# Third attention with scores first in a tick, second and last attention with the later weights split in eight pieces

## Chip, cores and metric

One core of a Trainium2 chip. The metric is the device time of one execution in microseconds: the median of the runs shown, and beside it one execution taken with the hardware profiler, on which all rows below rest. One launch computes everything.

## What is computed

The kernel runs twelve layers on an activation x of 64 sequences of 32 tokens with 256 features: four rounds of cross-attention, self-attention and feed-forward network. Each layer adds its result to x; all but the first pass of x are normalized (mean and variance over the 256 features) before a layer. The change touches three self-attentions. Each has 16 heads of 64 features:

```python
q = x @ Wq; k = x @ Wk; v = x @ Wv            # 256 -> 1024, all three
# second attention (l1a): biases on q, k, v and the output, causal mask
# third attention (l2a): own normalization gain and offset, q and k brought to length 1 in each head,
#   times a scale for each feature, scores times 8, a distance bias, causal,
#   two constant keys and values for each head ahead of the 32 tokens
# last attention (l3a): plain, softmax with 1e-10 added to the sum
scores = q k^T * scale ; p = softmax(scores) ; x = x + (p v) @ Wo
```

## The kernel before, in words

TensorE, VectorE, ScalarE, GpSimd and the SyncE queue each run a program written out by hand; they meet in semaphores only. x lies in the on-chip memory as 16 tiles of 128 tokens (four sequences each). A weight or activation that enters a precise product is taken apart in an upper part (rounded, written by ScalarE with `copy_act`) and a lower part (the difference, written by VectorE with a subtraction), and `three` issues three products for one: upper by upper, lower by upper, upper by lower.

**Ticks.** A layer's stages are ordered by `ticks(n, stages, order)` (L87): in tick t it calls, in the order of the list, each stage for tile t minus its lag; the lag is the key or the first entry of the key. Each engine has a list of its own. A wait blocks everything behind it on its engine.

**Banks.** `Banks.take` hands out PSUM banks in rotation; who takes a bank first waits until its contents of before have been read (`freed`). In the three attentions two banks rotate; scores have two banks of their own and values four.

**SelfAttention** (L899 to L1104), p is the lag of the scores: scores at p (TensorE); top at p on VectorE (mask, maximum, subtraction: L1034, L1039, L1041); exponential at p + 2 (ScalarE); divide at p + 3 (VectorE: L1047, L1052, L1054, then 32x32 turnings L1059, L1060); constant at p + 4 (TensorE, L976, third attention only: products of the constant values); values at p + 4 (TensorE, L991), then their result copied by ScalarE (first half of the heads, upper part) and VectorE (`outT`: L1070, L1074, L1076); project at p + 5 (TensorE, 24 products with the output weights), and total at p + 5 (VectorE: addition to x, L389, with statistics L374, L378), which also frees the bank of the projection. In the third attention the lower part of the values' result has a single buffer: `outT` waits for the projection of the tile before it, ahead of L1074.

**wide_attn** (L1246) is the second (`l1a`) and the last (`l3a`) attention, p = 2. Its weights come in seven loads; q and k are taken apart between the four groups of the normalization (`norm.act`, `norm.dve` with `upper` and `lower` as `between`, four units: two halves of q, two of k). Then each of ScalarE and VectorE takes apart the two halves of v (128x1024), ScalarE also the output weights (128x2048), before its first tick; VectorE's lower part of the output weights stands in `row` (tick 1). Two tiles make one group u for the products: `p1` with part "a" and "b" at lag 0 gives q in tick 2u and k in tick 2u + 1, two banks of 12 products for each part, and at lag 4 v. `evict` copies them out: in the second attention ScalarE the even and VectorE the odd banks of q and k (L1395, L1397), in the last the other way round (L200, L1393).

**l2_attn** (L1448) is the third attention, p = 3. For tile i, p1 "q" and "k" (lag 0) make q and k, two banks of 6 products each, p1v (lag 4) v, p2 "q" and "k" (lag 2) turn them on TensorE with the identity (L1548), constant at lag 7, values 7, project 8. VectorE at lag 0: copies q with its offset (L1646), sums of squares (L1649); GpSimd: `roots` (L1588, L1590), a power of -1/2; VectorE `p1b` at lag 1: q and k times the roots, one instruction (L1656, which the trace names g_xn); at lag 2 it copies the first half of the turned q and k (L1662), ScalarE the second (L1707); ScalarE also copies k (L200) and squares (L1696). TensorE's list is

```python
[(2, "q"), 3, (2, "k"), (7, "constant"), 8, (0, "k"), 7, (4, "v"), (0, "null"), (0, "q")]
```

VectorE's is `[2, 3, 8, 1, 6, (0, "k"), 7, (0, "q"), (0, "later")]`, where 3 is top, 8 total, 1 p1b, 6 divide, 7 outT.

## Time and profile before

| | |
|---|---|
| median of 3 runs | 3779.59 us (3779.45 to 3786.15) |
| profiled execution | 3792.68 us, span 3790.9 us |
| TensorE busy | 3426.5 us (90%), 39372 matmuls |
| VectorE busy | 2143.7 us (57%) |
| ScalarE busy | 1278.9 us (34%) |
| GpSimd busy | 900.4 us (24%) |
| granted clock of TensorE, mean | 0.938 |
| second attention | about 857 to 1122 us of the span |
| third attention | about 2108 to 2493 us |
| last attention | about 3489 to 3755 us |

A busy share is an average over twelve layers with different limits. A granted clock of 1.0 is the upper of TensorE's two levels (2.4 GHz), 0.5 the lower (1.2 GHz). Names: psum is the PSUM; l1a_, l2a_, l3a_ mark the tiles of the three attentions; g_ those of all layers.

### The profile page before, as it was taken

The numbers are of one execution on the slowest core, as the hardware profiler recorded it, in microseconds if no ns is written. First come the engines' busy times: TensorE is split into PE (matmuls) and PEld (weight loads), VectorE is DVE, ScalarE is ACT, GpSimd is POOL, SyncE is SP. The second block draws the span as 40 slices with busy tenths as digits, with TensorE's granted clock in tenths as the row PEclk, the third lists the DMA queues.
The fourth block names the chain that finished last, engine by engine and source line by source line (L and its number), as shares of the span: only waits on it lengthen the run. The fifth ranks groups of instructions, "written<-read, shape, count | busy, mean of one in ns | idle before, by whom it ended". The sixth has DMA issues, their size and how long they took to land.

```text
span 3790.9 us, 92569 instructions
## 1 busy us (share of the span) xinstructions
PE 3426.5 (90%) x39372; PEld 2774.3 (73%) x39372; DVE 2143.7 (57%) x5316; ACT 1278.9 (34%) x3193; POOL 900.4 (24%) x1393
## 2 busy tenths in 40 slices
PE   7988749988998889999999789889999999998996
PEld 6876647547986667777777577778888777776895
DVE  5756553356665165555555567654444466666467
ACT  5863101323212223333333443232232244445111
POOL 6657124122022332222222333100000111001102
PEclk9989769999997989999999899989999999998997
DMA  5620248531021321111110100021221111111000
GB/s 155 183 72 3 92 150 269 166 125 47 3 79 63 88 77 46 46 46 46 47 48 19 54 2 3 3 91 62 89 73 62 46 41 38 38 39 58 3 3 26
DMA packets 209995, 246.43 MB, mean 65 GB/s; under 512 B 18132, under 2 KB 189904, under 8 KB 206640
## 3 DMA queue, kind: packets, MB, share of 16 engines
q1 hardware_dynamic: 202096, 230.27, 19.1%
q0 software_dynamic: 7488, 10.23, 1.5%
q8 instruction: 313, 5.13, 0.5%
q14 instruction: 98, 0.80, 0.1%
HBM read 221.46 MB, written 18.61 MB: 63 GB/s over the span
## 4 chain that ended last, share of the span: by engine, by line
PE 71%; DVE 15%; issue 6%; ACT 3%; POOL 3%; DMA 1%; SPq 0%; ACTq 0%; POOLq 0%; DVEq 0%
PE psum L189 44%; PE psum L3621 10%; PE psum L991 2%; DVE l3x_P L3966 2%; PE psum L3100 1%; PE psum L963 1%; PE psum L3862 1%; PE psum L3201 1%; PE psum L3169 1%; PE psum L976 1%; DVE l3x_V L3949 1%; DVE l2a_ss L1649 1%; POOL l0a_ms L1191 1%; PE psum L3110 1%; DVE g_xn L258 1%
## 5 line engine op out<-in xcount | busy, mean ns | idle before, releaser
L3621 PE MATMUL psum<-l2f_hhi,l2f_whi 128*128 128x512 f32 x512 | 199.2, 389 | 0.0
L3621 PE MATMUL psum<-l2f_hlo,l2f_whi 128*128 128x512 f32 x512 | 199.2, 389 | 0.0
L3621 PE MATMUL psum<-l2f_hhi,l2f_wlo 128*128 128x512 f32 x512 | 199.2, 389 | 0.0
L245 POOL TENSOR_SCALAR g_rs<-g_mv 128x4 f32<-128x4 f32 x24 | 5.2, 218 | 778.2 <-DVE g_mv L378 777.7
L189 PE MATMUL psum<-l2x_kT,l2x_Qp 128*128 128x257 f32 x768 | 179.2, 383 | 2.6 <-ACT g_xn L3513 2.6
L189 PE MATMUL psum<-g_xn,l2x_tok 128*128 128x384 f32 x512 | 177.7, 489 | 1.4 <-ACT g_xn L3522 1.4
L189 PEld LDWEIGHTS psum<-l2x_kT,l2x_Qp 128*128 128x128 f32 x768 | 142.0, 191 | 21.7 <-issue 3.0
L3675 DVE CAST l2f_hhi<-l2f_tmp 128x512 fp32r<-128x512 f32 x96 | 41.0, 427 | 201.4 <-ACT l2f_tmp L3738 200.3
L189 PEld LDWEIGHTS psum<-g_xn,l2x_tok 128*128 128x128 f32 x512 | 93.3, 190 | 56.9 <-issue 2.6
L3949 DVE COPY l3x_V<-psum 128x512 f32<-128x512 f32 x64 | 44.3, 691 | 159.6 <-PE psum L189 159.6
L389 DVE TENSOR_TENSOR g_x<-g_x,psum 128x256 f32<-128x256 f32 x128 | 53.0, 415 | 132.2 <-PE psum L189 129.1
L3738 ACT ACTIVATE l2f_tmp<-psum,g_cols 128x512 f32<-128x512 f32 x64 | 44.2, 690 | 240.1 <-PE psum L3621 240.1
L200 ACT ACTIVATE l2x_Pc<-psum 128x384 f32<-128x384 f32 x128 | 62.8, 492 | 183.9 <-PE psum L189 183.9
L4022 ACT ACTIVATE l3x_P<-psum,l3x_sm 128x257 f32<-128x257 f32 x256 | 117.5, 469 | 16.0 <-DVE l3x_sm L3958 15.9
L189 PE MATMUL psum<-l3x_ctxT,l3x_wk 128*128 128x256 f32 x512 | 121.4, 380 | 0.0
L189 PE MATMUL psum<-l3x_wv,l3x_ctxT 128*128 128x256 f32 x512 | 121.0, 379 | 0.0
L3513 ACT ACTIVATE g_xn<-psum,l2x_sm 128x257 f32<-128x257 f32 x192 | 89.0, 472 | 90.8 <-DVE l2x_sm L3422 90.8
L3415 DVE TENSOR_REDUCE l2x_sm<-psum 128x3 f32<-128x771 f32 x64 | 61.5, 961 | 102.2 <-PE psum L189 102.2
L3621 PEld LDWEIGHTS psum<-l2f_hlo,l2f_whi 128*128 128x128 f32 x512 | 96.1, 188 | 20.2
L3621 PEld LDWEIGHTS psum<-l2f_hhi,l2f_whi 128*128 128x128 f32 x512 | 96.1, 188 | 19.9
L3621 PEld LDWEIGHTS psum<-l2f_hhi,l2f_wlo 128*128 128x128 f32 x512 | 96.1, 188 | 19.9
L200 ACT ACTIVATE l3x_PT<-psum 128x512 f32<-128x512 f32 x64 | 38.3, 598 | 207.4 <-PE psum L3862 207.4
(854 smaller groups left out, 10079.2 us busy)
## 6 DMA issues: line engine op xcount, KB each, us to landing
l2f_raw<-L2f_h SPq DMA_DIRECT2D x64, 512.0 KB, 3.2
l0f_w<-L0f_w SPq DMA_DIRECT2D x23, 1024.0 KB, 8.0
l0x_ctxT<-ctxT SPq DMA_DIRECT2D x64, 257.0 KB, 2.8
l1x_ctxT<-ctxT SPq DMA_DIRECT2D x64, 257.0 KB, 6.0
l0x_ctok<-ctx SPq DMA_DIRECT2D x64, 256.0 KB, 3.0
l1x_ctok<-ctx SPq DMA_DIRECT2D x64, 256.0 KB
l2x_cT<-ctxT SPq DMA_DIRECT2D x64, 256.0 KB, 2.7
l2x_tok<-ctx SPq DMA_DIRECT2D x128, 128.0 KB, 2.8
```

The lines of the kernel that those rows point to most:

```text
L189: ins = e.matmul(out, lhsT, rhs, start=start and n == 0, stop=stop and n == len(pairs) - 1, skip_group_check=skip)
L200: return e.activation(out, in_, ACT.Copy)
L389: e.tensor_tensor(K.x[:, i, :], K.x[:, i, :], part, ALU.add).then_inc(*K.sig("x").up())
L991: t = e.matmul(self.o_bank[j][par * hd:(par + 1) * hd, ch * 32:ch * 32 + 32], v[s, b * hd:(b + 1) * hd], PT[s, par * nch + ch, :], start=n ...
L3415: e.tensor_reduce(m(0), rows[:, :, 0:257], AX.X, ALU.max).then_inc(*s_top.up())
L3513: t = e.activation(P[k][:, n, :], bank[n][:, 0:257], ACT.Exp, bias=sm[:, k, 2, n:n + 1], scale=0.125, accum_out=sm[:, k, 3, n:n + 1])
L3621: t = e.matmul(z, a, b, start=c == 0 and u == 0, stop=c == 7 and u == 2)
L3675: e.tensor_copy(h[0][:, m, :], u[:]).then_inc(*h_hi.up())
L3738: e.activation(tmp[n % 4][:], banks.of(("m", g, n))[:], ACT.Gelu, scale=K.col(("L2_ffn_h1_s", "L2_ffn_h2_s")[n // 8], n % 8)).then_inc(*ge ...
L3949: e.tensor_copy(V[b % 6][:], banks.of(("v", b))[:].rearrange("p (k d) -> p k d", k=2)).then_inc(*v_ok.up())
L3966: t = e.tensor_scalar(P[b % 3][:, r, :], P[b % 3][:, r, :], m(0)[:, r:r + 1], None, ALU.mult)
L4022: e.activation(P[k][:, r, :], bank[r][:, 0:257], ACT.Exp, bias=sm[:, k, 1, r:r + 1], scale=0.25, accum_out=sm[:, k, 2, r:r + 1]).then_inc( ...
```

## The change

Three edits.

In the second and last attention the units of v and of the output weights become eight pieces of 512 columns (one `c` of the two, one half of the columns), and the engines take them apart inside the ticks: `later` calls `upper` or `lower` for two pieces in each of ticks 0 to 3, one after the first copies of products ("c"), one at the end of the tick ("d"). The loads stay as they were; the waits for the pieces (`w_lo.at(...)`) are counted anew.

In the third attention the lists of TensorE, VectorE and ScalarE are put in another order, and VectorE's copies of the turned q and k become two stages.

```diff
-        units = [(n, slice(h * 512, (h + 1) * 512)) for n in "qkv" for h in range(2)] + [("o", slice(0, 1024))]
+        half = [slice(h * 512, (h + 1) * 512) for h in range(2)]
+        units = [(n, slice(0, 2), half[h]) for n in "qk" for h in range(2)] + [(n, slice(c, c + 1), h) for n in "vo" for h in half for c in range(2)]
...
-                    w.wait_ge(w_lo.at(n // 2 + 1 if n < 8 else 5 + n % 2))
+                    w.wait_ge(w_lo.at(n // 2 + 1 if n < 8 else 6 + 2 * (n % 2)))
...
-            n, cols = units[u]
+            n, c, cols = units[u]
             w.wait_ge(w_hi.at(u + 1))
-            e.tensor_tensor(W[n][1][:, :, cols], raw[n][:, :, cols], W[n][0][:, :, cols], ALU.subtract).then_inc(*w_lo.up())
+            e.tensor_tensor(W[n][1][:, c, cols], raw[n][:, c, cols], W[n][0][:, c, cols], ALU.subtract).then_inc(*w_lo.up())
...
-            copy_act(e, W[n][0][:, :, cols], raw[n][:, :, cols]).then_inc(*w_hi.up())
+            copy_act(e, W[n][0][:, c, cols], raw[n][:, c, cols]).then_inc(*w_hi.up())
...
-        at.wo_ok = w_lo.at(7)
+        at.wo_ok = w_lo.at(12)
...  VectorE
-            for u in (4, 5):
-                lower(e, w, u)
+            def later(i, part):
+                if i < 4:
+                    lower(e, w, 4 + 2 * i + part)
...
-                lower(e, w, 6)
...
-            ticks(16, {**evict(e, w, banks, "dve"), (1, "row"): row, **at.dve(e, w, banks)}, [2, (0, "a"), (4, "a"), 5, 6, 7, (0, "b"), (4, "b"), (1, "row")])
+            ticks(16, {**evict(e, w, banks, "dve"), (1, "row"): row, (0, "c"): lambda i: later(i, 0), (0, "d"): lambda i: later(i, 1),
+                       **at.dve(e, w, banks)}, [2, (0, "a"), (4, "a"), (0, "c"), 5, 6, 7, (0, "b"), (4, "b"), (1, "row"), (0, "d")])
...  ScalarE
-            for u in (4, 5, 6):
-                upper(e, w, u)
...
+                  [(4, "power"), (0, "a"), (4, "a"), (0, "c"), 6, (0, "b"), (4, "b"), (0, "d")])
...  third attention, TensorE
-                  [(2, "q"), 3, (2, "k"), (7, "constant"), 8, (0, "k"), 7, (4, "v"), (0, "null"), (0, "q")])
+                  [3, (2, "q"), (7, "constant"), (2, "k"), 7, 8, (0, "k"), (4, "v"), (0, "null"), (0, "q")])
...  VectorE (p2 now takes q or k by its second argument)
-                  [2, 3, 8, 1, 6, (0, "k"), 7, (0, "q"), (0, "later")])
+                  [(2, "q"), 3, (2, "k"), 1, 7, 8, 6, (0, "k"), (0, "q"), (0, "later")])
...  ScalarE
-                       **at.act(e, w, banks)}, [2, 5, (0, "k"), 7, (4, "v"), (0, "q"), (0, "later")])
+                       **at.act(e, w, banks)}, [2, 5, 7, (0, "k"), (4, "v"), (0, "q"), (0, "later")])
```

## Rows read from the trace of the kernel before

**Rows 1.** The page: the chain that ended last, share of the span by engine.

```profile
PE 71%; DVE 15%; issue 6%; ACT 3%; POOL 3%; DMA 1%; SPq 0%; ACTq 0%; POOLq 0%; DVEq 0%
```

**Rows 2.** Table by windows: stretch, length, busy PE, PEld, DVE, ACT, POOL, PE clock, DMA.

```profile
2339.06:2358.59 19.53, 18.32 (x396) 15.62 (x396) 14.76 (x25) 7.46 (x12) 5.73 (x2) 1.00 0.01 3
```

**Rows 3.** Timeline of TensorE, one tick: start, length, instruction, idle before it.

```profile
2339.68 0.66 PE L1548 MATMUL psum<-g_ident,g_xn 128*128 128x128 f32 x4 [1.07 <-DVE g_xn L1646]
...
2341.73 1.09 PE L1548 MATMUL psum<-g_ident,g_xn 128*128 128x128 f32 x8 [0.17 <-DVE l2a_qT L1662]
...
2347.59 0.39 PE L189 MATMUL psum<-l2a_wkhi,g_xT_parts 128*128 128x512 f32 x1
...
2348.99 0.39 PE L189 MATMUL psum<-l2a_wkhi,g_xT_parts 128*128 128x512 f32 x1
...
2351.90 0.50 PE L189 MATMUL psum<-l2a_wvhi,g_xT_parts 128*128 128x512 f32 x1
```

**Rows 4.** Timeline of VectorE over the same tick.

```profile
2336.83 0.75 DVE L1646 SCALAR_TENSOR_TENSOR g_xn<-psum,l2a_qs,l2a_bq 128x512 f32<-128x512 f32 x1
...
2343.09 0.78 DVE L1034 SCALAR_TENSOR_TENSOR l2a_P<-psum,l2a_alibi 128x272 f32<-128x272 f32 x2
...
2347.79 0.42 DVE L389 TENSOR_TENSOR g_x<-g_x,psum 128x256 f32<-128x256 f32 x1 [2.41 <-PE psum L189]
...
2348.55 2.26 DVE L1656 TENSOR_TENSOR g_xn<-g_xn,l2a_ss 128x2048 f32<-128x2048 f32 x1
2350.72 0.71 DVE L1047 TENSOR_REDUCE l2a_nm<-l2a_P 128x16 f32<-128x544 f32 x1
...
2354.40 0.68 DVE L1070 CAST l2a_oThi<-psum 128x512 fp32r<-128x512 f32 x1
...
2356.37 0.75 DVE L1646 SCALAR_TENSOR_TENSOR g_xn<-psum,l2a_qs,l2a_bq 128x512 f32<-128x512 f32 x1
```

**Rows 5.** Timeline of GpSimd over the same tick.

```profile
2341.10 0.29 POOL L1588 TENSOR_SCALAR l2a_ss<-l2a_ss 128x32 f32<-128x32 f32 x1 [13.70 <-DVE l2a_ss L1649]
2341.47 5.44 POOL L1590 TENSOR_TENSOR l2a_ss<-l2a_ss,g_negh 128x32 f32<-128x32 f32 x1
```

**Rows 6.** Timeline of GpSimd, other ticks, and the table by windows over one.

```profile
2190.52 5.44 POOL L1590 TENSOR_TENSOR l2a_ss<-l2a_ss,g_negh 128x32 f32<-128x32 f32 x1
2204.22 5.46 POOL L1590 TENSOR_TENSOR l2a_ss<-l2a_ss,g_negh 128x32 f32<-128x32 f32 x1
...
2239.18 5.45 POOL L1590 TENSOR_TENSOR l2a_ss<-l2a_ss,g_negh 128x32 f32<-128x32 f32 x1
2261.18 5.44 POOL L1590 TENSOR_TENSOR l2a_ss<-l2a_ss,g_negh 128x32 f32<-128x32 f32 x1
...
2240.00:2260.00 20.00, 18.31 (x269) 15.62 (x268) 13.06 (x20) 6.77 (x11) 4.63 (x1) 0.91 0.01 2
```

**Rows 7.** Second attention: timelines of TensorE, ScalarE, VectorE, and one window.

```profile
874.54 0.55 PE L189 MATMUL psum<-g_xT_parts,l1a_wqhi 128*128 128x256 f32 x1 [6.98 <-ACT l1a_q L1395]
...
868.28 2.03 ACT L200 ACTIVATE l1a_wvhi<-l1a_wv 128x1024 fp32r<-128x1024 f32 x2
...
873.57 0.82 ACT L1395 ACTIVATE l1a_q<-psum,g_cols 128x256 f32<-128x256 f32 x2
...
870.60 2.35 DVE L1367 TENSOR_TENSOR l1a_wv_parts<-l1a_wv,l1a_wvhi 128x1024 fp32r<-128x1024 f32 x2
...
874.50:879.10 4.60, 4.56 (x22) 4.59 (x23) 0.00 (x0) 0.84 (x2) 0.00 (x0) 0.52 0.00 0
```

**Rows 8.** Last attention: timelines of VectorE and TensorE, and one window.

```profile
3502.13 2.35 DVE L1367 TENSOR_TENSOR l3a_wv_parts<-l3a_wv,l3a_wvhi 128x1024 fp32r<-128x1024 f32 x2
...
3505.23 0.55 PE L189 MATMUL psum<-g_xT_parts,l3a_wqhi 128*128 128x256 f32 x1 [6.04 <-DVE l3a_q L1393]
...
3505.20:3510.60 5.40, 5.37 (x25) 5.40 (x26) 0.69 (x1) 1.26 (x2) 0.00 (x0) 0.50 0.00 0
```

**Rows 9.** Waits in 2105 to 2500 us: engine, line, releaser, total, times, longest.

```profile
PE psum L976 <- DVE l2a_oTlo L1076: 9.7, 4, 4.0
```

More of the change, by code:

```diff
@@ L1293, in sp @@
             mark["w"] = wt.now()
-            for u, (n, cols) in enumerate(units[:6]):
+            for u in range(6):
+                n, cols = "qkv"[u // 2], half[u % 2]
                 load(e, w_in[u], raw[n][:, :, cols], A[pre + "_" + n].rearrange("(c p) m -> p c m", p=128)[:, :, cols])
@@ L1363, in lower @@
         def lower(e, w, u):
-            n, cols = units[u]
+            n, c, cols = units[u]
             w.wait_ge(w_hi.at(u + 1))
-            e.tensor_tensor(W[n][1][:, :, cols], raw[n][:, :, cols], W[n][0][:, :, cols], ALU.subtract).then_inc(*w_lo.up())
+            e.tensor_tensor(W[n][1][:, c, cols], raw[n][:, c, cols], W[n][0][:, c, cols], ALU.subtract).then_inc(*w_lo.up())
         def upper(e, w, u):
-            n, cols = units[u]
-            w.wait_ge(w_in[u].at(2 if n == "o" else 1))
-            copy_act(e, W[n][0][:, :, cols], raw[n][:, :, cols]).then_inc(*w_hi.up())
-        at.wo_ok = w_lo.at(7)
+            n, c, cols = units[u]
+            w.wait_ge(w_in[6].at(2) if n == "o" else w_in[2 * "qkv".index(n) + cols.start // 512].at(1))
+            copy_act(e, W[n][0][:, c, cols], raw[n][:, c, cols]).then_inc(*w_hi.up())
+        at.wo_ok = w_lo.at(12)
         def evict(e, w, banks, mine):
@@ L1432, in act, with later @@
             w.wait_ge(L("cols").at(0))
-            for u in (4, 5, 6):
-                upper(e, w, u)
-            ticks(16, {**evict(e, w, banks, "act"), **{(4, "power") if k == 4 else k: f for k, f in at.act(e, w, banks).items()}}, [(4, "power"), (0, "a"), (4, "a"), 6, (0, "b"), (4, "b")])
+            def later(i, part):
+                if i < 4:
+                    upper(e, w, 4 + 2 * i + part)
+            ticks(16, {**evict(e, w, banks, "act"), **{(4, "power") if k == 4 else k: f for k, f in at.act(e, w, banks).items()},
+                       (0, "c"): lambda i: later(i, 0), (0, "d"): lambda i: later(i, 1)},
+                  [(4, "power"), (0, "a"), (4, "a"), (0, "c"), 6, (0, "b"), (4, "b"), (0, "d")])
         K.layer(sp, pe, pool, dve, act)
@@ L1656, in p1b, with p2 @@
                 e.tensor_tensor(d, d, f.unsqueeze(2).to_broadcast([128, 32, 64]), ALU.mult).then_inc(*qn_ok.up())
-            def p2(i):
-                for n in (0, 2):
+            def p2(i, a):
+                for n in [2 * a]:
                     w.wait_ge(turned.at(4 * i + n + 1))
-                    o = (qT[i % 2][:].rearrange("p c (j q) -> p c j q", j=4), kT[i % 2][:, :, :, 2:34])[n // 2]
+                    o = (qT[i % 2][:].rearrange("p c (j q) -> p c j q", j=4), kT[i % 2][:, :, :, 2:34])[a]
                     e.tensor_scalar(o[:, 0:4], banks.of(("T", i, n))[:].rearrange("p (c j q) -> p c j q", c=4, j=4),
                                     K.col(("L2_attn_q_scale", "L2_attn_k_scale")[n // 2], 0), None, ALU.mult).then_inc(*T_dve.up())
-            ticks(16, {(0, "q"): lambda i: p1(i, 0), (0, "k"): lambda i: p1(i, 1), 1: p1b, 2: p2,
-                       (0, "later"): later, **at.dve(e, w, banks)},
-                  [2, 3, 8, 1, 6, (0, "k"), 7, (0, "q"), (0, "later")])
+            ticks(16, {(0, "q"): lambda i: p1(i, 0), (0, "k"): lambda i: p1(i, 1), 1: p1b,
+                       (2, "q"): lambda i: p2(i, 0), (2, "k"): lambda i: p2(i, 1), (0, "later"): later, **at.dve(e, w, banks)},
+                  [(2, "q"), 3, (2, "k"), 1, 7, 8, 6, (0, "k"), (0, "q"), (0, "later")])
         def act(e):
```

## Prediction

> **What bounds the kernel now.** I read the page first, then split the stage of the third attention (2105 to 2493 us of the span) into its ticks with the table by windows, then the timelines of VectorE, TensorE and GpSimd over one tick, and last the first microseconds of the second and the last attention. The chain that ended last is mostly TensorE [rows 1], so a change counts where it moves TensorE's waits. A full tick of the third attention takes 19.53 us, of which TensorE is busy 18.3 and VectorE 14.8, at the full clock (2.4 GHz) [rows 2]. TensorE's two waits in it are 1.07 us, before the second half of the turning of q, for VectorE's copy of q's second half, and 0.17 us before the turning of k [rows 3]. Its work without them is 19.53 - 1.07 - 0.17 = 18.3 us.
>
> In the second attention TensorE stands 6.98 us after its first 24 products, until ScalarE's copy of q ends [rows 7]; in the last it stands 6.04 us, until VectorE's [rows 8]. In both cases the copy is late because the engine first takes apart all the later weights.
>
> **Third attention, part by part.** The change moves work only; no instruction is added here, and no DMA moves. On TensorE scores now stand ahead of the turning of q (they last about 1.3 us, the time between the turnings that start at 2339.68 and 2341.73 less the first of them and the wait [rows 3], and so cover the 1.07), the constant part stands between the turnings (it covers the 0.17), and values come ahead of the output projection. If nothing else waited the tick would be 18.3 us.
>
> But VectorE's order changes too: the big multiplication by the roots (L1656), then the three copies of the values' result, then the addition to x (L389). Before, the addition came ahead of the multiplication, 2347.79 against 2348.55 [rows 4]. The multiplication needs GpSimd's roots, and these end at 2341.47 + 5.44 = 2346.91 [rows 5], 1.64 us before it began: not waited for today. And the addition frees the bank (there are two) which the second half of k's product takes: banks are taken as q, q, k, k (turnings), y, k, k, v, v, q, q, so that product takes y's bank. The new order closes a loop over four engines. Its length, from the rows:
> - second half of k's product to the first copy of q: 2356.37 - 2348.99 = 7.38, less the values, which move out of it, 2351.90 - 2348.99 - (2348.99 - 2347.59) = 1.51: 5.87 us [rows 3, 4];
> - first copy of q to the start of the roots, 2341.10 - 2336.83 = 4.27, and to their end 5.81 more [rows 4, 5];
> - multiplication until the next instruction starts, 2350.72 - 2348.55 = 2.17; copies of the values' result, 2356.37 - 2354.40 = 1.97; the addition 0.42 [rows 4]; some 0.13 for three signals between engines.
> Sum 5.87 + 4.27 + 5.81 + 2.17 + 1.97 + 0.42 + 0.13 = 20.64 us against 19.54: +1.1 us per tick, and TensorE's stand moves to the second half of k's product, where it is 20.64 - 18.3 = 2.3 us. VectorE itself stands some 2.3 us for the roots in the same tick. Eight ticks have both a k and a y (8 to 15): 8 x 1.1 = **+8.8 us**.
>
> First ticks. Where no y is taken yet, k's product takes the bank of the turned k, which VectorE now copies after the mask, maximum and subtraction (2.3 us: from 2343.09 to 2347.79 less the 2.41 of standing [rows 4]) instead of before. Chain from the first copy of q: 4.1 to the copy of the turned q, which starts just before the roots' 4.27; 0.7 + 2.3 + 0.75 for it, the softmax's top and the turned k's copy; then k, v and half of q at 1.40 us a half: 5 x 1.40, and 0.25 for signals: 15.1 us. The shortest such tick now is 2204.22 - 2190.52 = 13.7 us [rows 6]. Of the five ticks 3 to 7 I count two as bound so, those with v and without divide and values; in the others something else is as long: 2 x 1.4 = **+2.8**, between 0 (if the mask waits are shorter) and 7 (all five).
>
> Last ticks (16 to 23). Today TensorE stands up to 4.0 us for the lower copy of the values' result [rows 9]. In the new order that copy waits, with its single buffer, for the projection before it, which is now issued after values; so 1.3 us of it come into each of some five ticks, less one projection that no longer waits at the very end (3.3), and less 0.65 a tick of the copy's first part that gets out of the chain. Bounds -3 and +6, taken **+3**, nearer to the chain's rows. Sum for the third attention +14.6.
>
> TensorE's clock. One of the eight ticks took 22.0 us instead of 19.54 (roots at 2239.18 and 2261.18), with a granted clock of 0.91 over it: part of it ran at the lower level (1.2 GHz) [rows 6]. A slow stretch that falls between scores and the first half of k would now be covered by the 2.3 us stand; against that, the new stand may bring slow stretches of its own. I let the two cancel, with -4 and +11 as bounds.
>
> **Second attention.** ScalarE now ends its part of the normalization at 868.28, where it began the v weights, and copies q at once instead of at 873.57 [rows 7]. The copy frees TensorE 0.97 us after its start: 869.25 instead of 874.54. The next half waits for VectorE, which is free at 870.60: copy 0.85 as ScalarE's, so 871.5, and 24 products end by 873.0. Before, they began at 874.54 and, at the lower clock (0.52 in the row that covers them), ended at 879.1 [rows 7]. Gain 6.1. The later stages are bound by TensorE, so it stays. The single piece of 2.3 us that delays the first softmax afterwards becomes 0.7: 0.4 more. **-6.5 us.**
>
> **Last attention.** VectorE copies q where it began the two v pieces (3502.13), and not after them: 2.3 us of 2.35 [rows 8]. The first 24 products after the stand took 5.4 us at a granted clock of 0.50 [rows 8], 2.8 at the full one. With a stand of 3.8 instead of 6.0 us the fall may or may not come: 0 to 2.5, taken 1.0. **-3.3 us**, between -2.3 and -4.8.
>
> The pieces: eight of 512 columns where there were two of 1024 and one of 2048. Two of 1024 take 2.35 us on VectorE [rows 7], so a piece of 512 costs at most half a 1024 and its fixed part, some 0.7: 5.5 against 4.6 us, in stretches where TensorE is behind with the products that VectorE copies. A piece waits for ScalarE's, and behind it stand a copy and then the softmax; the copy has the length of a half product (1.4) to spare. Cost 0, at worst 0.5 a tick over four ticks in two stages, +4.
>
> **Sum.** +14.6 - 6.5 - 3.3 = +4.8 us, against the profiled execution's 3792.7 (span 3790.9): 3797.5. The runs' median stands 13 us lower, and I carry the difference over: 3779.6 + 4.8 = **3784 us**.
>
> **Rivals.**
> Scores first pays in full: the roots are not in the loop (GpSimd's spans are rough), or the addition to x does not hold k's bank. Then ticks of 18.3: 8 x -1.2, and -3 at the end, -12.6 in all, -22.4 with the other stages: 3757 us. For it: VectorE has 4.7 us to spare in a tick [rows 2]. Against it: five ticks show the same 5.44 to 5.46 us for the roots [rows 5, 6].
>
> Slower by the clock. This is the case that ends on the other side of no change. The place is the second half of k's product: TensorE stands 2.3 us there in one piece, and v and q come next. It decides if that stand, once a tick, lets the clock fall: then the products behind it, which are in the loop, lose 1.4 us on average a tick, 8 x 1.4 = +11: 3795 us. For it: the tick of 22.0 us [rows 6]; against it: with a stand of 1.07 the clock was 1.00 [rows 2]. The Trainium skill ("TensorE: Matmul & The Clock Gate", section on a second failure mode, PSUM-queue depth-cycling) says that short stands between groups of products, made by cycling through PSUM banks, can make the clock oscillate; by it this case would be the likeliest.
>
> The pieces do little: copies are held up behind them and the clock falls in the last attention all the same. Then 5 us are gained there and not 9.8: 3789 us.
>
> **How the numbers follow.** Forecast 0.60 (a total between 3776 and 3792 by the bounds), scores pay 0.12, clock 0.15, pieces 0.13. About 0.2% (7.6 us) is what a measurement of this kernel can tell from no change. Faster by more: the second case, and 0.02 of the first: 0.14. Slower: clock 0.15, half of the pieces' case, and 0.13 of the forecast's own: 0.35. Within: 0.51. The range 3769 to 3796 leaves out most of the second case and the end of the third.
>
> **What would show it.** In ticks 8 to 15 of the third attention: start to start 20.6 us; TensorE waits some 2.3 us at a product of k for VectorE's addition L389, none for L1646; VectorE's L1656 waits some 2.3 us for GpSimd. In the second attention TensorE's first stand 2 us and a second of 0.9, in the last 3.8. Wrong, if the ticks are 18.3 or over 21.5 us, or L1656 is not waited for.

## The result: 0.34% slower, and the profile after

The changed kernel takes 3795.0 us (median of 17 runs, 3786.17 to 3808.68) against 3781.4 us for the kernel before measured beside it (17 runs, 3773.79 to 3790.45). The ratio is 1.0034, 95% interval 1.0025 to 1.0044: slower by 9 to 17 us. The forecast was 3784 us in a range of 3769 to 3796, so the time lies inside the range, but only 1 us from its upper end, and on the side that had a chance of 0.35; that no change beyond the noise would be seen had been the likelier case, with 0.51.

The profiled execution of after (span 3786.8 us) happens to be shorter than that of before (3790.9 us), and this must not be read as a gain. The code that neither kernel changed took 2890.6 us in the profile of before and 2878.1 us in that of after; in the fourteen profiles of this study it lies anywhere from 2874.3 to 2890.6 us. So I compare the three stages themselves. Each is measured by the starts of two instructions that are in every trace:

| stage, from and to | before | after | difference |
|---|---|---|---|
| second attention: first product of q to the logits' addition | 864.5 to 1135.4: 270.9 | 855.0 to 1117.7: 262.7 | -8.2 |
| third attention: first roots to the last addition to x (L389) | 2130.3 to 2490.9: 360.6 | 2112.2 to 2495.35: 383.1 | +22.5 |
| last attention: first product of q to the first instruction on l3f_wi | 3496.1 to 3764.9: 268.8 | 3497.9 to 3760.8: 262.9 | -5.9 |
| the rest of the span | 2890.6 | 2878.1 | -12.5, by chance |

The three stages add up to +8.4 us in this pair of profiles. A second profile of after, taken on another chip (run e8 below), has 262.9, 388.3 and 265.4 us: +16.3. The measured 9 to 17 us lie around these. The stages scatter too: the third attention took 383.1 and 388.3 us in the two profiles of after, and 356.4 to 363.8 us in the five profiles with the old order (before, e2, e10, e11, e12), so a single pair of profiles is good to some 5 to 7 us only.

The page's chain of after, to be read against [rows 1] (shares of the span by engine):

```profile
PE 73%; DVE 15%; issue 4%; POOL 4%; ACT 3%; DMA 1%; SPq 0%; ACTq 0%; DVEq 0%; POOLq 0%
```

GpSimd went from 3 to 4% of the chain: its roots (L1600) are now on it, with 2%.

Two ticks of the third attention after, by the table by windows (stretch, length, busy PE, PEld, DVE, ACT, POOL, granted clock, DMA), cut at the starts of the roots, as an answer to [rows 2]:

```profile
2250.10:2272.10 22.00, 19.70 (x404) 16.66 (x403) 14.75 (x24) 7.44 (x12) 5.73 (x3) 0.92 0.01 2
...
2316.40:2337.00 20.60, 18.27 (x407) 15.55 (x403) 14.69 (x25) 7.44 (x12) 5.75 (x2) 1.00 0.01 2
2337.00:2359.10 22.10, 19.80 (x404) 16.68 (x404) 14.67 (x25) 7.44 (x12) 5.72 (x2) 0.92 0.01 2
2359.10:2379.80 20.70, 18.42 (x408) 15.61 (x404) 14.78 (x25) 7.44 (x12) 5.75 (x2) 1.00 0.01 2
```

There are two kinds of full ticks, and a first one apart. Where the granted clock is 1.00 over the whole tick it takes 20.6 us, the length of the loop that the prediction worked out (20.64). Where it is 0.92, TensorE does the same work in 19.8 instead of 18.3 us and the tick takes 22.1 us: the whole 1.5 us is paid. The first full tick, 22.92 us, is another matter: over it the clock was 0.81 and TensorE busy for 22.5 us, so it hardly stood at all, and its low clock set the tick; the low clock came at the start, 0.55 over the first 9.7 us. Over the eight full ticks the starts of the roots are 22.92, 21.99, 22.17, 22.05, 20.62, 22.15, 20.64 and 20.61 us apart (before: 22.00, 21.68, 19.55, 19.54, 19.52, 19.54, 19.53, 19.86).

The loop itself can be followed in the timeline of one such tick after (start, length, engine, line, instruction, idle before it and what ended it), which answers to [rows 3], [rows 4] and [rows 5]. TensorE's rows first:

```profile
2357.05 1.09 PE L1558 MATMUL psum<-g_ident,g_xn 128*128 128x128 f32 x8
2358.08 1.99 PE L976 MATMUL psum<-l2a_PnT,l2a_nv 32*128 32x32 f32 x64
2359.99 1.09 PE L1558 MATMUL psum<-g_ident,g_xn 128*128 128x128 f32 x8
...
2369.27 0.50 PE L189 MATMUL psum<-l2a_wkhi,g_xT_parts 128*128 128x512 f32 x1 [1.44 <-DVE g_x L389]
```

VectorE and GpSimd over the tick:

```profile
2358.64 0.74 DVE L1672 TENSOR_SCALAR l2a_qT<-psum,g_cols 128x512 f32<-128x512 f32 x1
2359.18 5.46 POOL L1600 TENSOR_TENSOR l2a_ss<-l2a_ss,g_negh 128x32 f32<-128x32 f32 x1
...
2364.67 2.29 DVE L1666 TENSOR_TENSOR g_xn<-g_xn,l2a_ss 128x2048 f32<-128x2048 f32 x1 [2.42 <-POOL l2a_ss L1600]
2366.88 0.68 DVE L1070 CAST l2a_oThi<-psum 128x512 fp32r<-128x512 f32 x1
2367.60 0.69 DVE L1074 TENSOR_TENSOR l2a_oTlo<-psum,l2a_oThi 128x512 fp32r<-128x512 f32 x1
2368.20 0.68 DVE L1076 TENSOR_TENSOR l2a_oTlo<-psum,l2a_oThi 128x512 fp32r<-128x512 f32 x1
2368.80 0.41 DVE L389 TENSOR_TENSOR g_x<-g_x,psum 128x256 f32<-128x256 f32 x1
...
2375.18 0.75 DVE L1656 SCALAR_TENSOR_TENSOR g_xn<-psum,l2a_qs,l2a_bq 128x512 f32<-128x512 f32 x1 [1.89 <-PE psum L189]
```

What the change set out to do is there: the two turnings have no wait in front of them, and the constant's products lie between them. Then VectorE stands 2.42 us for GpSimd's roots, works without a gap through multiplication, three copies and addition, and only when the addition has run does TensorE go on with the second half of k's product (2369.27; the stand is 1.44 us here, with another of 0.84 us earlier in the tick, ahead of the projection, and 2.30 in one piece in the tick before). That product leads to the next copy of q (2375.18), and this one to the next roots: the loop is closed.

In the four ticks at 0.92, and in e1's two, the clock falls at the end of this stand or within 1.2 us behind it. Four stretches of after by the table by windows: in the tick of 22.1 us TensorE is idle, then 2 us later at the lower clock; in the tick of 20.6 us before it the same stand is followed by the upper clock:

```profile
2345.00:2347.00 2.00, 0.00 (x0) 0.00 (x0) 1.97 (x5) 1.06 (x2) 0.00 (x0) 1.00 0.00 0
2349.00:2352.00 3.00, 3.00 (x9) 2.32 (x8) 2.08 (x5) 1.63 (x3) 0.00 (x0) 0.50 0.00 0
```

```profile
2324.00:2326.00 2.00, 0.16 (x1) 0.00 (x0) 1.97 (x4) 1.23 (x2) 0.00 (x0) 1.00 0.00 0
2328.00:2331.00 3.00, 3.00 (x14) 2.44 (x13) 2.47 (x5) 1.84 (x4) 0.00 (x0) 1.00 0.00 0
```

The list of waits of after over 2100 to 2510 us (engine, line, releaser, total, times, longest; PEld is TensorE's loading of weights, which meets the same stand):

```profile
DVE g_xn L1666 <- POOL l2a_ss L1600: 39.2, 16, 5.3
...
PEld psum L189 <- DVE g_x L389: 22.1, 12, 2.8
PE psum L189 <- DVE g_x L389: 16.9, 12, 2.3
...
PE psum L976 <- DVE l2a_PT L1060: 11.9, 4, 4.7
```

In the same list of before there is no wait of TensorE's product for L389 at all, and VectorE waited for the roots 6 times, 12.7 us. The four waits of [rows 9], for the lower copy of the values' result, are gone, and four for the turned softmax weights (L1060), of up to 4.7 us, stand in their place.

The second attention after, timelines of ScalarE, VectorE and TensorE, against [rows 7]:

```profile
858.11 0.87 ACT L1397 ACTIVATE l1a_q<-psum,g_cols 128x256 f32<-128x256 f32 x2
...
860.43 0.87 DVE L1399 TENSOR_SCALAR l1a_q<-psum,g_cols 128x256 f32<-128x256 f32 x2
861.22 0.68 DVE L1369 TENSOR_TENSOR l1a_wv_parts<-l1a_wv,l1a_wvhi 128x512 fp32r<-128x512 f32 x1
861.35 0.38 PE L189 MATMUL psum<-g_xT_parts,l1a_wqhi 128*128 128x256 f32 x1 [0.58 <-DVE l1a_q L1399]
```

And the last attention after, TensorE, against [rows 8]:

```profile
3504.00 0.36 PE L189 MATMUL psum<-g_xT_parts,l3a_wqhi 128*128 128x256 f32 x1 [1.01 <-DVE l3a_q L1395]
```

The stands of 6.98 and 6.04 us have shrunk to 0.58 and 1.01 us. Here the first 24 products of q ran partly at the lower clock (0.50 over the first 2 us in the second attention and the first 4 us in the last), and covered part of the wait themselves; in runs where they ran at the full clock the stands are 1.7 and 0.6 us in the second attention and 3.76 us in the last (below).

One part of the old stand is not a conversion. ScalarE, which TensorE waited for in the second attention, itself stood for the load of the output weights before it took them apart, between the v weights of [rows 7] and its copy of q:

```profile
871.76 1.91 ACT L200 ACTIVATE l1a_wohi<-l1a_wo 128x2048 fp32r<-128x2048 f32 x1 [1.45 <-DMA l1a_wo<-L1a_o]
```

So of the 5.3 us by which the copy came later than ScalarE could have begun it, 1.45 were a wait for a transfer. Putting the weights off takes this wait out of the way as well.

### The profile page after: what moved, and what is told of

Its sections match the earlier page's. It is cut to its first block, busy times and chain, and to the rows that moved or that the text cites. A ratio compares the mean times of both kernels' runs of the same rounds, so it can differ in the third digit from the quotient of the medians.

```text
span 3786.8 us, 92604 instructions
## 1 busy us (share of the span) xinstructions
PE 3414.4 (90%) x39372; PEld 2763.8 (73%) x39372; DVE 2145.4 (57%) x5326; ACT 1279.3 (34%) x3203; POOL 901.6 (24%) x1393
## 4 chain that ended last, share of the span: by engine, by line
PE 73%; DVE 15%; issue 4%; POOL 4%; ACT 3%; DMA 1%; SPq 0%; ACTq 0%; DVEq 0%; POOLq 0%
PE psum L189 46%; PE psum L3631 10%; PE psum L991 2%; DVE l3x_P L3976 2%; POOL l2a_ss L1600 2%; PE psum L963 1%; PE psum L3110 1%; PE psum L3872 1%; PE psum L3211 1%; PE psum L3179 1%; DVE l3x_V L3959 1%; DVE g_xn L258 1%; POOL l0a_ms L1191 1%; PE psum L3120 1%; PE psum L3111 1%
## 5 line engine op out<-in xcount | busy, mean ns | idle before, releaser
L3924 POOL COPY l3x_kT<-l3x_kTt 128x2 f32<-128x2 f32 x64 | 12.3, 192 | 402.8 <-PE psum L3863 392.4
```

## The experiments

They go from the change's two halves (e1, e2) to the loop (e3 to e5), to better orders (e6, e7), to a repeat of the whole (e8), to the clock (e9), and to what in the pieces does the work (e10 to e12). Every ratio is to the kernel before, run beside it on the same chip.

**e1: only the third attention.** The functions of the second and last attention are those of before.

> Only the new orders of the third attention; the first, second and last attention as before. Theory: the change is a loss of the third attention and a gain of the pieces. The profile of after shows the third attention 22.6 us longer (383.2 us against 360.6 us), so this kernel should be 18 to 24 us slower than before, with ticks of 20.6 and of 22.1 us. Rival: the pieces change nothing of their own and the third attention is all there is; then it is 10 to 16 us slower, like the whole change.

Measured: 3804.75 us against 3783.1, ratio 1.0051 (1.0035 to 1.0068), +19 us. The stage takes 379.9 us (+19.3 over before); the second and the last attention are as before (269.5, 267.0 us). The full ticks are 22.83, 22.15, 20.59, 20.57, 20.62, 20.57, 21.74 and 20.60 us. The theory holds in its middle value: the third attention alone loses more than the whole change does. The two intervals overlap (0.35 to 0.68% against 0.25 to 0.44%), so this run by itself does not exclude the rival; that the pieces gain on their own, which e2 and e12 show, does. The same loop of 20.6 us is there, but the clock was 0.92 in two of the seven ticks behind the first (22.15 and 21.74 us), against four in after, though the code of the stage is the same.

**e2: only the pieces.** The third attention is that of before.

> Only the later weights in eight pieces; the third attention as before. Theory: the second attention shrinks by 8.1 us and the last by 5.9 us, as between the two profiles, and this kernel is 10 to 14 us faster than before. Rival of the prediction's own sizes: 6.5 + 3.3, 10 us. Rival: the stands only move and the clock takes back what they gave; 0 to 5 us faster.

Measured: 3767.98 us against 3783.1, ratio 0.9956 (0.9944 to 0.9969), -17 us, more than any of the three expectations. In its profile the second attention takes 266.1 and the last 267.0 us. The question of the size is taken up with e12.

**e3: half of the roots.** One edit in after:

```diff
-                e.tensor_tensor(f, f, K.negh[:, 0:32], ALU.pow).then_inc(*rs_ok.up())
+                e.tensor_tensor(f[:, 0:16], f[:, 0:16], K.negh[:, 0:16], ALU.pow).then_inc(*rs_ok.up())
```

> After, with GpSimd taking roots of 16 of the 32 columns (those of q's norms; the norms of k are used without root, so this part of the result is left out). The roots take 2.7 to 3 us in place of 5.8. Theory: the roots stand in the loop that sets the tick (k's second half, copy of q, roots, multiplication, copies, addition); then the middle ticks fall from 20.6 and 22.1 us to 18.5 to 19 us, the wait of VectorE's multiplication for GpSimd from 5.3 us to under 2 us, and the kernel is 20 to 30 us faster than after. Rival: the tick is set by TensorE's order and its lower clock, and the roots have slack; then the ticks stay within 0.5 us and the kernel gains under 8 us, in its first ticks alone.

Measured: 3773.92 us, ratio 0.9964 (0.9952 to 0.9977); against after (1.0034) that is 0.70%, 26 us faster. From its trace, first the roots themselves (duration least, median, most), then the waits:

```profile
L1600 POOL TENSOR_TENSOR l2a_ss<-l2a_ss,g_negh x16: 2907/2925/3920, 2116.8 to 2380.5; 128x16 f32<-128x16 f32 x16
```

```profile
PEld psum L189 <- DVE g_x L389: 9.8, 12, 0.8
...
DVE g_xn L1666 <- POOL l2a_ss L1600: 3.0, 2, 2.8
```

The roots shrink by 2.5 us. Five of the full ticks take 18.66 to 18.69 us: 1.95 us less than 20.6, and there they come near TensorE's own 18.3 us of work. VectorE's wait for the roots all but vanishes, and TensorE's for the addition shrinks from up to 2.8 to at most 0.8 us. The roots are in the loop.

**e4: the addition ahead of the multiplication.** After, with one list changed, VectorE's:

```diff
-                  [(2, "q"), 3, (2, "k"), 1, 7, 8, 6, (0, "k"), (0, "q"), (0, "later")])
+                  [(2, "q"), 3, (2, "k"), 7, 8, 1, 6, (0, "k"), (0, "q"), (0, "later")])
```

> After, with one list changed: in VectorE's order the addition (7) and its successor (8) stand ahead of the multiplication (1) that waits for GpSimd's roots, with everything else as it is. Theory: the addition, which TensorE's second half of the product of k waits for, then no longer stands behind the roots; the loop is opened, the wait of TensorE for the addition (2.3 us, 12 times) is gone or under 1 us, the ticks are 18.7 to 19.5 us, and the kernel is 12 to 20 us faster than after. Rival: the multiplication's own consumers (the turnings) are just as urgent and the wait only moves to them: under 5 us.

Measured: 3777.2 us (11 runs), ratio 0.9986 (0.9978 to 0.9995); 0.48%, 18 us, faster than after. The starts of the roots in its full ticks and its waits:

```profile
2238.70 5.44 POOL L1600 TENSOR_TENSOR l2a_ss<-l2a_ss,g_negh 128x32 f32<-128x32 f32 x1
2257.52 5.45 POOL L1600 TENSOR_TENSOR l2a_ss<-l2a_ss,g_negh 128x32 f32<-128x32 f32 x1
2276.29 5.43 POOL L1600 TENSOR_TENSOR l2a_ss<-l2a_ss,g_negh 128x32 f32<-128x32 f32 x1
```

```profile
DVE g_xn L1666 <- POOL l2a_ss L1600: 16.5, 6, 5.3
...
PE psum L189 <- DVE g_x L389: 4.6, 12, 0.4
```

Six of the eight full ticks take 18.7 to 18.8 us (the last two 19.5 and 20.2), the roots last as long as ever, and VectorE waits for them as rarely as in the kernel before. So the loop needs two links, the roots and the place of the addition behind them, and either alone opens it. The work is that of after, instruction for instruction; only its order on one engine differs.

**e5: half of the roots in the kernel before.** The edit of e3, in the old order.

> The control of the run on the roots: the kernel before, with GpSimd's roots on 16 of 32 columns (the norms of k without root, so this part of the result is left out). Theory: before, the roots had slack in the full ticks and set only the first ones; the full ticks stay at 19.5 to 19.6 us, the first ones shrink, 5 to 12 us faster than before in all. Rival: the roots set the tick in every order, and shorter ones are worth 20 us or more here too.

Measured: 3773.27 us against 3782.8, ratio 0.9975 (0.9957 to 0.9992), -10 us. The later full ticks stay at 19.53 to 19.58 us, where before had 19.52 to 19.55; the ticks before them are shorter. So before, the roots had slack in a full tick, as [rows 5] said: the change took it away.

**e6: a part of TensorE's new order.** The pieces, and before's third attention with one list changed, TensorE's:

```diff
-                  [(2, "q"), 3, (2, "k"), (7, "constant"), 8, (0, "k"), 7, (4, "v"), (0, "null"), (0, "q")])
+                  [3, (2, "q"), (7, "constant"), (2, "k"), 8, (0, "k"), 7, (4, "v"), (0, "null"), (0, "q")])
```

> The pieces, and of the third attention only a part of TensorE's new order: the scores go first and the constant's products between the turnings of q and k, but the other values' products (7) stay behind the first half of the product of k, and the lists of VectorE and ScalarE are the old ones. Theory: these two moves are good in themselves, ticks of 18.6 to 19 us, 5 to 15 us faster than the pieces alone, so 20 to 30 us faster than before; what cost the time is (7) ahead of the product of k together with the addition behind the roots. Rival: the scores first are the loss; the ticks are 19.6 us or more and the kernel gains nothing on the pieces alone.

Measured: 3766.84 us against 3782.8, ratio 0.9949 (0.9930 to 0.9968), -19 us; with 0.85% less than after the lowest ratio of the study, though its interval overlaps those of the pieces alone (e2: 0.9944 to 0.9969, e12: 0.9954 to 0.9983). That it beats these is shown by its stage, not by its time. The stage takes 347.6 us, 13.0 less than before (e2 and e12: 363.8 and 356.4):

```profile
2248.43 5.43 POOL L1600 TENSOR_TENSOR l2a_ss<-l2a_ss,g_negh 128x32 f32<-128x32 f32 x1
2267.14 5.45 POOL L1600 TENSOR_TENSOR l2a_ss<-l2a_ss,g_negh 128x32 f32<-128x32 f32 x1
2285.83 5.43 POOL L1600 TENSOR_TENSOR l2a_ss<-l2a_ss,g_negh 128x32 f32<-128x32 f32 x1
```

Seven of the eight full ticks take 18.6 to 18.7 us (the last, at a clock of 0.92, 20.4). The change's title idea, the scores first and the constant's products between the turnings, is a good one. What turned it into a loss is the rest of the reordering. In the full ticks that is the addition behind the roots, as e4 shows. e4 keeps the rest and has nearly these ticks, but its stage takes 360.9 us, 13 more than e6's: 8 of them lie behind the last roots (96.3 against 88.4 us) and 4 in the first seven intervals (112.3 against 108.1). So the other moves cost too, above all in the last ticks; which of them does it (the values' products ahead of the product of k, or the lists of VectorE and ScalarE) was not tried one by one. The whole run gained 19 us by its ratio, with an interval of 12 to 26; 13 us here and 9 to 14 for the pieces (below) make 22 to 27, which this interval largely covers.

**e7: both out of the loop.** After with three other lists:

```diff
-                  [3, (2, "q"), (7, "constant"), (2, "k"), 7, 8, (0, "k"), (4, "v"), (0, "null"), (0, "q")])
+                  [(7, "constant"), (2, "q"), 3, (2, "k"), 7, 8, (0, "k"), (4, "v"), (0, "null"), (0, "q")])
...
-                  [(2, "q"), 3, (2, "k"), 1, 7, 8, 6, (0, "k"), (0, "q"), (0, "later")])
+                  [(2, "q"), (2, "k"), 6, 3, 8, 7, (0, "k"), 1, (0, "q"), (0, "later")])
...
-                       **at.act(e, w, banks)}, [2, 5, 7, (0, "k"), (4, "v"), (0, "q"), (0, "later")])
+                       **at.act(e, w, banks)}, [2, 7, 5, (0, "k"), (4, "v"), (0, "q"), (0, "later")])
```

> After with three other lists in the third attention: TensorE takes the constant's products ahead of the turning of q; VectorE takes both copies of the turned tiles and its part of the exponents' sums first, then the scores' maximum, the addition (8 and 7), k's copy, and the multiplication that waits for the roots as late as it can; ScalarE takes its part of 7 ahead of 5. Theory: neither the roots nor the addition stand in the loop, TensorE's own work sets the tick at 18.0 to 18.5 us, and the kernel is 20 to 32 us faster than before, the fastest of all. Rival: the turnings then wait for the late multiplication, ticks as in the run with the addition first (18.8 us) or longer, and 6 us or less faster than before.

Measured: 3777.26 us, ratio 0.9984 (0.9970 to 0.9998): my theory of it was wrong, its rival right. The full ticks are uneven, 19.02 to 22.24 us. Two of them in the table by windows:

```profile
2344.00:2366.20 22.20, 19.64 (x407) 17.14 (x404) 14.90 (x25) 7.40 (x13) 5.73 (x2) 0.92 0.01 2
2305.20:2324.30 19.10, 18.27 (x415) 15.77 (x415) 15.03 (x25) 7.52 (x13) 5.78 (x3) 1.00 0.01 3
```

and one of its waits, which after's list does not have:

```profile
PEld psum L1558 <- DVE g_xn L1666: 12.2, 4, 6.7
```

The turnings now wait for the multiplication that I put late, and the clock was at 0.92 in three of the ticks. It is no better than e4.

**e8: after once more**, unchanged, on the chip of e5 to e7.

> After, unchanged, beside the others on one chip. The third attention alone cost 0.51% and the pieces alone gave 0.44%, which would add to 0.07% (3 us); the whole change measured 0.34% (13 us). If the two parts add, this run comes out 0 to 8 us slower than before and the first measurement was at its edge; if they disturb each other (ticks of 22.1 us in place of 20.6 in the third attention), it is 10 to 17 us slower again.

Measured: 3795.9 us (12 runs) against 3782.8, ratio 1.0029 (1.0015 to 1.0044), 11 us slower: the first result stands. Whether the two parts of the change add up can't be told from the times: e1 (0.51%) with e2 (0.44%) would give 0.07%, below this interval of 0.15 to 0.44%, but with e12's 0.31% for the pieces it gives 0.20%, inside it. Its full ticks are 22.91, 21.99, 22.19, 22.09, 20.63, 22.16, 20.63 and 20.62 us, within 0.04 us the pattern of the first profile.

**e9: the stand filled with useless work.** After, with eight more products a tick, whose result is thrown away:

```diff
                     cols = slice((n % 2) * 512, (n % 2 + 1) * 512)
+                    if n == 2:
+                        matmuls(e, z[:], [(norm.parts(c, i * 128, (i + 1) * 128)[h], W["k"][0][:, c, cols]) for c in range(2) for h in range(2)] * 2)
                     three(e, z[:],
```

> After, with eight extra products of TensorE in each tick of the third attention, ahead of the first half of the product of k and into its own bank (the real products then begin anew there), about 1.9 us of useless work. In the full ticks of after, TensorE stands 2.3 us behind that first half for the addition, and in five of seven of these ticks the granted clock falls (0.92 for the tick) and the tick takes 22.1 us, against 20.6 where it stays at 1.00. Theory: the loop of 20.6 us is set elsewhere, the stand is what makes the clock fall; with the stand filled TensorE waits under 0.6 us there, the clock stays at 1.00, the ticks are all 20.6 to 21 us, and the kernel is 3 to 10 us faster than after although it does more. Rival: the extra products lie on the path (the first half's copy comes 1.9 us later); then each tick grows by up to 1.9 us and the kernel is 10 to 25 us slower than after.

Measured: 3801.83 us, ratio 1.0061 (1.0041 to 1.0080), 0.27% or 10 us slower than after in the middle values; its interval overlaps that of after (to 1.0044), and its stage of 390.5 us stands against 383.1 and 388.3 in the two profiles of after. So the gain that I forecast did not come, while a loss is hardly shown. In the full ticks the theory came out:

```profile
2280.00:2301.10 21.10, 20.19 (x395) 17.11 (x391) 14.74 (x25) 7.45 (x12) 5.74 (x2) 1.00 0.01 2
...
2323.00:2343.60 20.60, 20.12 (x412) 17.04 (x408) 14.69 (x25) 7.45 (x12) 5.72 (x3) 1.00 0.01 2
2343.60:2364.20 20.60, 20.15 (x414) 17.07 (x410) 14.70 (x25) 7.45 (x12) 5.72 (x2) 1.00 0.01 2
```

```profile
PE psum L189 <- DVE g_x L389: 3.5, 8, 0.6
```

TensorE does 1.85 us more work in a tick than in after's 20.6 us ones (20.12 against 18.27), the clock is 1.00 over each, four of them are no longer than the loop, and the eight of them take 167.6 us where after took 173.2: more work, 5.5 us less time. But the seven intervals ahead of them grew from 115.1 to 126.2 us, and took back more than that. Where I had reckoned with full ticks only, the early ones decided.

**e10 and e11: putting off without cutting, cutting without putting off.** Both with before's third attention. e10 keeps the units of before (two halves of v, the output weights whole) and takes them in the first two ticks; the core of it, written against after (ScalarE likewise):

```diff
-        units = [(n, slice(0, 2), half[h]) for n in "qk" for h in range(2)] + [(n, slice(c, c + 1), h) for n in "vo" for h in half for c in range(2)]
+        units = [(n, slice(0, 2), half[h]) for n in "qk" for h in range(2)] + [("v", slice(0, 2), h) for h in half] + [("o", slice(0, 2), slice(0, 1024))]
...
-                if i < 4:
-                    lower(e, w, 4 + 2 * i + part)
+                if 2 * i + part in (0, 1, 3):
+                    lower(e, w, 4 + i + part)
```

> The third attention as before; the later weights put off into the first ticks but not cut: v's two halves in the first tick, the output weights whole in the second. Theory: what the pieces bring is that the conversions no longer stand ahead of the first copies of q's product, and the cut hardly matters; 8 to 16 us faster than before, within 4 us of the eight pieces. Rival: a conversion of 2.35 or 1.9 us ahead of the copies makes TensorE stand again; half of the gain or less is left.

e11 keeps the eight pieces and takes them where before does; on VectorE, again against after:

```diff
-            def later(i, part):
-
-                if i < 4:
-                    lower(e, w, 4 + 2 * i + part)
+            for u in range(4, 8):
+                lower(e, w, u)
...
+                for u in range(8, 12):
+                    lower(e, w, u)
```

> The third attention as before; the later weights cut in eight but taken apart where the kernel before does it (ahead of the first tick, the output weights' lower parts at its end). Theory: the cut alone brings nothing; TensorE's stands of 7.0 us and 6.0 us at the first products of q remain and the time is within 4 us of before. Rival: smaller pieces let ScalarE and VectorE work side by side and the stands shrink by 2 us or more each.

Measured: e10 3773.16 us against 3783.34, ratio 0.9975 (0.9963 to 0.9988), -9.5 us; e11 3786.86 us, ratio 1.0014 (0.9999 to 1.0030). TensorE's stands at the start of the second and of the last attention, from the timelines, first e10's:

```profile
855.25 0.36 PE L189 MATMUL psum<-g_xT_parts,l1a_wqhi 128*128 128x256 f32 x1 [1.72 <-ACT l1a_q L1397]
857.49 0.39 PE L189 MATMUL psum<-g_xT_parts,l1a_wqhi 128*128 128x256 f32 x1 [0.59 <-DVE l1a_q L1399]
...
3482.62 0.55 PE L189 MATMUL psum<-g_xT_parts,l3a_wqhi 128*128 128x256 f32 x1 [3.76 <-DVE l3a_q L1395]
```

then e11's:

```profile
869.79 0.55 PE L189 MATMUL psum<-g_xT_parts,l1a_wqhi 128*128 128x256 f32 x1 [7.29 <-ACT l1a_q L1397]
...
3503.09 0.55 PE L189 MATMUL psum<-g_xT_parts,l3a_wqhi 128*128 128x256 f32 x1 [6.17 <-DVE l3a_q L1395]
```

Putting off is what brings the time; the cut alone brings nothing, and its stands are even 0.3 and 0.1 us longer than before's: ScalarE's eight pieces take 4.4 us in the second attention, the three old ones 3.9. Its two stages are longer as well, 275.8 and 273.1 us. With the weights put off, the cut adds 2 us (e12 against e10, 3770.8 and 3773.2), which the intervals don't separate from nothing. The stages leave this open too: e10's take 265.5 and 268.1 us, and the last one, where the stand is the same 3.76 us with and without the cut, is no shorter than with the old edit (268.6 in the mean, below). One profile is too little to say whether the cut helps there.

**e12: the pieces alone once more.**

> The eight pieces alone once more, beside the two variants of it. The stage lengths of the profiles so far with the pieces are shorter by 5.0 us in the second attention and 3.2 us in the last (means of seven profiles against three), 8 us together, near the 9.8 us of the prediction; the first measurement of the pieces alone gave 0.44%, 16 us. If the stages say all of it, this run comes out 6 to 12 us faster than before; if 14 us or more, part of the gain lies outside these two stages.

Measured: 3770.8 us against 3783.34, ratio 0.9969 (0.9954 to 0.9983), -12 us. Its second and last attention take 260.5 and 265.1 us. The two measurements of the pieces, 0.44 and 0.31%, overlap and have their middle at 14 us. The means of the profiles are: second attention 263.5 us with late pieces of eight (nine profiles, after and e2 to e4, e6 to e9, e12) against 269.2 with the old edit (before, e1, e5), last attention 265.5 against 268.6. So the stages show 5.7 + 3.1 = 8.8 us. Whether the other 5 us are real, outside the two stages, or the scatter of the unchanged rest stays open; the interval of e12 (5 to 17 us) takes in 8.8, that of e2 (12 to 21) does not.

## Why the prediction was right in its mechanism and short in its sum

**The loop of 20.64 us: right.** Ticks with the clock at 1.00 take 20.57 to 20.64 us in after, e1 and e8. Each of the two links was tried alone: half the roots (e3) and the addition first (e4) bring the tick to 18.7 and 18.8 us, and the same halving leaves the old order's full ticks at 19.5 (e5). The waits foretold are there: TensorE for L389, 2.3 us, and VectorE for GpSimd, 2.4 us, and none for the copies of q in a full tick. The term of +8.8 us measures 8 x (20.62 - 19.54) = 8.6 us. The prediction named ticks over 21.5 us as a sign of being wrong, and five of the eight are: by that sign the loop is not the whole account of the ticks, and the clock, next, is what it leaves out.

**"I let the two cancel": this step failed.** It gave the clock nothing, and the clock took part of the difference. In after five of eight full ticks are above 21.5 us, and the excess over the loop adds up to 173.15 - 8 x 20.62 = 8.2 us; before, two ticks were so, 161.22 - 8 x 19.54 = 4.9 us. The clock's net share is +3.3 us in this pair. The rival "slower by the clock" said that the stand of 2.3 us brings the fall, at 1.4 us a tick in each of eight. The price is right (1.5 us, the tick of 0.92 against that of 1.00). For the cause, count the full ticks behind the first whose clock is below 1.00: with the stand of 2.3 us ten of 21 (four each in after and e8, two in e1); in the old order, where TensorE's longest stand in a steady full tick is 1.07 us, four of 42 (before, e2, e5, e10, e11, e12); with the stand filled (e9) or shortened to 0.4 us (e3, e4) none of 21. So the stand makes the falls frequent, but it is not their only cause. The first full tick of after is not explained by it: TensorE hardly stands in it, and the clock is low from its start. Such a tick is there at 0.84 in e3 too (22.04 us), and was there before (22.00 us), yet not in e4 (18.72 us) and e9 (20.64 us); what brings it stays open. So the rival's mechanism came true in half of its ticks, beside the forecast's, and the same code had only two of them in e1. The section of the Trainium skill that the prediction set against its own sum ("TensorE: Matmul & The Clock Gate", on the second failure mode, PSUM-queue depth-cycling) named a danger that came true in part: the trace agrees in the ticks of 22.1 us, at 0.92, and not in those of 20.6 us, at 1.00 with the same stand.

**First ticks, +2.8: too small.** The first seven intervals took 108.9 us before and 115.1 after, +6.2. Of the five ticks I counted two as lengthened, at 1.4 us each. Of the first seven, three grew, 14.38, 16.36 and 13.70 us becoming 16.30, 18.96 and 16.60: by 1.9, 2.6 and 2.9. The bound of 7 that the prediction kept for all five holds it, but "in the others something else is as long" was a guess without a row. The chain itself was right: the fifth of these intervals, one of the two counted, takes 15.00 us in e1 and 15.07 in e4, where the clock over it is 1.00, against 15.1 worked out; in after it is 16.60 at 0.90. So the clock has a part in these ticks as well.

**Last ticks, +3: measured +4.4** from the last roots to the last addition (90.5 to 94.9 us). The waits for the lower copy are gone, as foretold, and those of up to 4.7 us for the turned softmax weights (L1060) stand there in their place; the prediction had not seen these. In e8 the same stretch took 99.9 us, at a mean clock of 0.80 against 0.84 in after, so part of this term is the clock again.

Together the third attention gives 8.6 + 3.3 + 6.2 + 4.4 = 22.5 us where the prediction had 14.6. In e1, which holds nothing else, the ratio says 19 us. The split depends on the pair. By the means of three profiles with the new order (after, e1, e8) and five with the old one (before, e2, e10, e11, e12) it is 8.6 for the loop, 3.0 for the clock, 5.0 for the first ticks and 6.6 for the last ones: 23.3 us.

**Second attention, -6.5:** -8.2 in the first pair of profiles, -5.7 in the means: right. Its two stands were put at 2 and 0.9 us and are 1.7 and 0.6. **Last attention, -3.3:** -5.9 in the first pair, -3.1 in the means: right, the stand of 3.8 us is 3.76. The open question of the clock is answered as well: it fell to 0.50 in or behind that stand in each of the nine profiles that have it, and stayed at 1.00 behind the 1.7 and 0.6 us of the second attention in each of the seven that have these. **Pieces at nothing:** the cut by itself measures between nothing and 0.3% (e11), and with late weights it is no loss (e12 against e10). The prediction gave the whole gain to the copies no longer standing behind the conversions, and e10 and e11 say the same by their times. It overlooked that 1.45 us of the stand were ScalarE's wait for a load; the sum is not touched, since it started from the time at which ScalarE was ready.

**The sum:** +4.8 foretold, 13 measured; the stages' means give 23.3 - 5.7 - 3.1 = 14.5. The mis-sized term is the third attention, by 5 to 9 us: its last ticks, the clock and its first ticks, by some 2 to 4 us each in the means, all on the same side. That the time still fell into the range, 1 us from its end, is in part luck. Two readings of the prediction are slightly off without touching the sum: by the rows it names the scores last 1.22 us, not 1.3, and the 0.91 is of 20 of the 22.0 us of that tick, which has 0.92.

## What to carry to other kernels

When engines work through hand-written lists, follow every instruction that is moved behind a slow one to what it sets free: a buffer's release behind a wait for another engine closes a loop whose length is the period, however idle each engine is. Sum such a loop from rows, then look which single link is the cheapest to take out; here it is one swap in one list (18 us), or taking over only two moves of TensorE's list and leaving the other lists alone (e6, faster than both kernels). And a stand that a list puts into TensorE's work once a period may cost twice, as waiting and as lower clock behind it. Where it cannot be removed, useful work from elsewhere in the period could fill it; that was not tried here, only useless work in every tick (e9), which helped in the full ticks and lost in the others.

## What the runs showed of the hardware that was not expected

The falls of the clock can repeat closely: in two profiles of after on different chips the eight full ticks agree within 0.04 us (22.92 and 22.91, 21.99 and 21.99, 22.17 and 22.19, 22.05 and 22.09, 20.62 and 20.63, 22.15 and 22.16, 20.64 and 20.63, 20.61 and 20.62). But this is no rule. e2 and e12 are one program too, also on two chips, and their full ticks begin with 21.75 and 23.50 us (0.92 and 0.85) in the one and 20.48 and 20.12 us (both 1.00) in the other, and sum to 164.8 and 157.9 us. And with other weights' code some 1000 us ahead of it (e1), the stage of after with the same stand of up to 2.3 us was at 1.00 in five of the seven ticks behind the first, where after was in three. So a stand of this length can pass without a fall. What decides in which tick one comes was not tried.

More work can take less time in a stretch: with 1.85 us of thrown away products in each, e9's eight full ticks took 5.5 us less than after's (2.3 of it in the first, which was 22.92 us and became 20.64), though the whole kernel did not gain.

The code that is the same in all kernels varied by 16 us between single profiles, as much as the effect that was looked for. A single pair of profiles would have said that the change is 4 us faster.
